# Attention's expert pieces: four raw buffers and loads two blocks ahead

## The reference, cut to what matters

```python
xn = _layernorm(x)
# spiking attention
Q, K, V = (spike(layer_norm(xn @ W.T + b, g, beta) - 1) for each of q, k, v)   # 16 heads of 16
attn = Dh - (q_sum + k_sum - 2 q k) + log_pe_bias(N, N)
out = spike(einsum(attn * scale, V) - 0.5)
attention = spike(layer_norm(out @ Wo.T + bo, go, betao) - 1)
# experts: 8, of which each token takes its best two
gate = renormalised top-2 of softmax(xn @ router_w.T)
experts = sum_e gate[e] * (silu(up_a) * up_b) @ down[e]
```

## Time and profile before

| | |
|---|---|
| three runs | 416.29 us median (415.83 to 416.88) |
| profiled execution | 416.35 us, of which 414.6 are the span from the first to the last instruction |
| TensorE busy | 364.6 us, 88% |
| TensorE weight loads | 298.1 us, 72% |
| VectorE busy | 271.8 us, 66% |
| GpSimd busy | 233.5 us, 56% |
| ScalarE busy | 225.4 us, 54% |
| granted clock of TensorE, mean | 0.957 (1.00 from 128 us to 400 us) |
| moved by the DMA engines | 51.72 MB, mean 125 GB/s |

### The profile page before, as it was taken

How to read it: one execution, slowest core, us unless ns; L and a number is a source line. 1 busy time by engine, 2 the same in 40 slices (tenths; PEclk the granted TensorE clock), 3 DMA queues, 4 the chain that set the end, 5 groups by cost and what they waited for, 6 DMA issues and landing times.

```text
span 414.6 us, 9181 instructions
## 1 busy us (share of the span) xinstructions
PE 364.6 (88%) x2421; PEld 298.1 (72%) x2430; DVE 271.8 (66%) x897; ACT 225.4 (54%) x716; POOL 233.5 (56%) x208
## 2 busy tenths in 40 slices
PE   5298976989999998988878999999999999999980
PEld 1233676988888856756667888888888888888860
DVE  4699799997776645856776555555555555555540
ACT  1456774777777654533444455555555555555540
POOL 4637423777777671644235657656555656565652
PEclk9589868999999999999999999999999999999996
DMA  7942012244534423466647566666666666665743
GB/s 264 323 155 77 25 51 53 104 156 130 176 136 162 159 104 102 146 197 212 174 142 227 81 113 102 102 102 103 102 102 101 103 100 104 99 105 93 112 52 38
DMA packets 43460, 51.72 MB, mean 125 GB/s; under 512 B 6342, under 2 KB 37064, under 8 KB 43432
## 3 DMA queue, kind: packets, MB, share of 16 engines
q0 software_dynamic: 13952, 19.30, 26.3%
q1 hardware_dynamic: 27488, 30.21, 24.5%
q10 hardware_dynamic: 1992, 1.89, 1.4%
HBM read 27.89 MB, written 23.48 MB: 124 GB/s over the span
## 4 chain that ended last, share of the span: by engine, by line
PE 54%; DVE 19%; issue 10%; POOL 6%; ACT 5%; DMA 4%; SPq 1%; POOLq 1%; DVEq 0%; ACTq 0%
PE bank L1137 15%; PE bank L1139 14%; PE bank L1138 14%; POOL rstd L704 4%; PE bank L1282 3%; PE bank L1264 3%; DMA xn<-x 3%; DVE qk_spk L1006 3%; DVE xn L808 2%; ACT junk L486 2%; DVE xst L786 2%; POOL slot_x L688 2%; PE bank L1203 1%; PE bank L1318 1%; DMA ex<-slot_x 1%
## 5 line engine op out<-in xcount | busy, mean ns | idle before, releaser
L737 POOL DMA_INDIRECT out<-ey,dest x71 | 110.0, 1549 | 72.4 <-ACT ey L547 25.5
L684 POOL DMA_INDIRECT slot_x<-xn,pos x64 | 62.8, 982 | 26.0 <-issue 20.2
L1037 DVE TENSOR_TENSOR hid<-gact,bank 128x256 f32<-128x256 f32 x71 | 29.9, 421 | 69.8 <-ACT gact L531 69.8
L1137 PE MATMUL bank<-ew,exT_h 128*128 x142 | 62.1, 438 | 2.7 <-DVE exT_l L975 2.6
L1137 PE MATMUL bank<-w_h,xT_h 128*128 128x256 f32 x192 | 59.5, 310 | 0.1
L1138 PE MATMUL bank<-w_l,xT_h 128*128 128x256 f32 x192 | 56.6, 295 | 0.0
L1139 PE MATMUL bank<-w_h,xT_l 128*128 128x256 f32 x192 | 56.4, 294 | 0.0
L1139 PE MATMUL bank<-ew,exT_l 128*128 x142 | 55.9, 393 | 0.0
L1138 PE MATMUL bank<-ew,exT_h 128*128 x142 | 55.8, 393 | 0.0
L531 ACT ACTIVATE gact<-bank 128x256 f32<-128x256 f32 x71 | 27.2, 384 | 51.3 <-PE bank L1139 51.3
L486 ACT ACTIVATE junk<-bank 128x256 bf16<-128x256 f32 x96 | 35.9, 380 | 28.9 <-PE bank L1139 28.9
(11 more groups left out here) (204 smaller groups left out, 891.1 us busy)
## 6 DMA issues: line engine op xcount, KB each, us to landing
ex<-slot_x SPq DMA_DIRECT2D x71, 130.0 KB, 2.5
ew_f<-experts SPq DMA_DIRECT2D x24, 256.0 KB, 3.1
xo<-x SPq DMA_DIRECT2D x16, 256.0 KB, 3.0
out<-xo SPq DMA_DIRECT2D x16, 256.0 KB, 3.4
xn<-x SPq DMA_DIRECT2D x6, 512.0 KB, 12.3
out<-ey,dest POOLq DMA_INDIRECT x71, 3.8
xn<-x SPq DMA_DIRECT2D x4, 256.0 KB, 3.7
w_f<-w_all ACTq DMA_DIRECT2D x1, 1024.0 KB, 7.9
```

Source lines behind the costliest of these rows:

```text
L684: pool.indirect_dma_start(slot_x, bass.IndirectOffsetOnAxis(ap=pos[:, k, t:t + 1], axis=0), xn[:, t, :], None).then_inc(s[done], 16)
L737: pool.indirect_dma_start(out, bass.IndirectOffsetOnAxis(ap=dest[:, j:j + 1], axis=0), ey[:, j % 4, :], None, compute_op=ALU.add).then_inc ...
L1037: v.tensor_tensor(hid[:, m % 2, :], gact[:, m % 2, :], h_ps[m % 2][:, F:2 * F], ALU.mult).then_inc(s["hid_done"], 1)
L1137: mm(dst, a_h, b_h, start=first, stop=False)
```

## The change

Attention's pieces get four raw places in place of two. The two new ones, `ew_more`, lie over the projections' weights; `ey` moves behind them, onto the old raw places. Pieces k 0, 1, 4, 5, 8 and 9 of attention use the old places, k 2, 3, 6 and 7 the new ones, each place with a semaphore of its own. SP issues k 0 in step 0 and k 1 in step 1 as before, k 2 and k 3 in step 2 after a wait for the last projection, k 4 and k 5 in step 3, and from step 4 on piece a+2 in step a; from k 4 on each waits until the piece four back is subtracted. All these issues stand in front of the step's wait for a store and its load of x, where `load_late` stood behind x.

```diff
+        ew_more = place_in(r_a)("ew_more", [P, 2, PW])
         ey = put("ey", [P, 4, D])
...
-        piece_in = [sem(f"piece_in{i}") for i in range(2)]
+        piece_in = [sem(f"piece_in{i}") for i in range(4)]
...
+        first_in_attention = POOL_PIECES + len(LATE_PIECES)
+
+        def raw_piece(n):
+
+            k = n - first_in_attention
+            if k >= 0 and k % 4 >= 2:
+                return ew_more[:, k % 2, :], piece_in[2 + k % 2], 16 * (k // 4 + 1)
+            earlier = n // 2 if k < 0 else first_in_attention // 2 + k // 4
+            return ew_f[:, n % 2, :], piece_in[n % 2], 16 * (earlier + 1)
...
+            def load_ahead(k):
+                n = ATTENTION_PIECES[k]
+                dst, done, _ = raw_piece(n)
+                if k < 2:
+                    sp.wait_ge(s["piece_l"], n - 1 - POOL_PIECES)
+                elif k >= 4:
+                    sp.wait_ge(s["piece_l"], n - 3 - POOL_PIECES)
+                sp.dma_start(dst, pieces[:, n]).then_inc(done, 16)
+
             sp.wait_ge(s["scattered_more"], 16 * TOPK * (FREED_MORE - FREED))
             for a in range(NB):
+                if a == 2:
+                    sp.wait_ge(s["proj_done"], G3 * NT)
+                for k in {0: [0], 1: [1], 2: [2, 3], 3: [4, 5]}.get(a, [a + 2]):
+                    if k in ATTENTION_PIECES:
+                        load_ahead(k)
                 if a >= 4:
                     sp.wait_ge(out_done[a % 4], 16 * (a // 4))
                 sp.dma_start(xo[:, a % 4, :, :], x_pairs[:, a, :, :]).then_inc(x_back[a % 4], 16)
-                if a in ATTENTION_PIECES:
-                    load_late(ATTENTION_PIECES[a])
                 if a >= 3:
                     store_block(a - 3)
...
             def piece_upper(n):
-                u = n % 2
+                raw, loaded, count = raw_piece(n)
...
-                act.wait_ge(piece_in[u], 16 * (n // 2 + 1))
-                nc.scalar.activation(piece(n, 0), ew_f[:, u, :], ACT.Copy).then_inc(s["piece_h"], 1)
+                act.wait_ge(loaded, count)
+                nc.scalar.activation(piece(n, 0), raw, ACT.Copy).then_inc(s["piece_h"], 1)
...
-                v.tensor_tensor(piece(n, 1), ew_f[:, m % 2, :], piece(n, 0).bitcast(F32), ALU.subtract).then_inc(s["piece_l"], 1)
+                v.tensor_tensor(piece(n, 1), raw_piece(n)[0], piece(n, 0).bitcast(F32), ALU.subtract).then_inc(s["piece_l"], 1)
```

## The result

Over seven runs of each, the changed kernel takes 410.99 us (median; 409.33 to 413.63) and the kernel before 415.83 (413.0 to 416.88). The ratio is 0.9891, with a 95% interval of 0.9855 to 0.9927: 4.5 us faster, between 3.0 and 6.0. The forecast was 411.5, range 410.6 to 413.2.

The account below looks back on a forecast made before the run. Late 256 KB piece loads, queued on SP behind a store's landing and x, were taken to hold ScalarE, VectorE and TensorE. Span 414.6 - 4.83 + 1.75 around it = 411.5 us; own range 410.6 to 412.4, given up to 413.2.

Parts of the forecast that it names:

- The four steps: Attention blocks 9 to 12: with no late piece, TensorE's steps shrink from 19.09 to 14.26 us, a gain of 4.83.
- The 0.85 at the end of attention: TensorE's idle time at 212.82, ascribed to the last blocks' own chain; none counted as gain, 0.85 possible at most.
- Two raw places over the weights, waits in front of x: SP queue: loads of k 2 and 3 wait for the last projection, x and stores behind moved waits; cost nothing.
- The landing of a store with a piece behind it: SP queue in attention: taken as 3.5 us, bounds 3.14 and 4.20; puts expert tile 4 at 212.1, cost 0 to 0.9.
- Ring order: Inside the DMA engines: by the skill's rule a piece behind a store would not hold it; landing 3.14, sum the same.
- L: The landing time of a store with a piece right behind it on the SP queue, taken as 3.5 us.
- The experts' stretch moves as a whole: Experts' 170 us, TensorE busy for 169.30: the stretch keeps its length and begins sooner.
- The rival in which SP's stores take the gain back: SP's out_done wait ahead of x becomes the bound, tile 4 turned 2.7 us later: 419.0 us, chance 0.05.

Follow-up runs that it names:

- the changed kernel's third profile: Changed kernel unchanged, run a second time in the experiments beside other kernels: 440.12 us against 446.14 for the kernel before, ratio 0.9855.
- the order alone: Kernel before with its two raw places; only the load of piece k moved in front of step k's store wait and load of x: ratio 0.9938.
- the lead alone: Changed kernel with four places and two blocks of lead, but piece loads behind x of their step: ratio 1.0012.
- The load behind the store: Kernel before, with the load of piece k behind the step's store instead of in front of it: ratio 0.9944.
- the end of attention tightened: VectorE's spike and tile parts reordered, tile 4 before the wait, zero rows earlier: on the changed kernel 0.9805; with two places and order alone 0.9804.
- VectorE's order at the end of attention: Changed kernel with block 15's spike before spike_out(12), and lower parts of expert tiles 0 and 1 before spike_out(13), on VectorE: ratio 0.9873.
- lead alone, tile 4 earlier: Four places and two-block lead with loads behind x, plus expert tile 4 issued in step 15 in front of the wait: ratio 0.9964.

## Why the prediction was right

- **The four steps.** Forecast 4.83 us from the earlier trace rows and 4.81 from the earlier trace rows; measured 4.84. All waits of L449 went, nothing took their place, VectorE and ScalarE had 2.9 and 2.0 us of work in steps of 3.6. The 0.85 at the end of attention stayed, 0.84 in the changed kernel, as forecast. It is less of a chain of its own than the prediction made it: the spike of block 15 stood on VectorE behind `spike_out` of block 12, which waits for the power, and with the spike in front the gap was gone.
- **Two raw places over the weights, waits in front of x.** Costed at nothing. Block 13 to the first expert matmul is 14.03 against 14.04 us; x of block 3 left at 162.19, in the time of the profile before 163.9, forecast near 164.
- **The landing of a store with a piece behind it.** Forecast 3.5 with 3.14 and 4.20 as ends; measured 2.87, 3.53 and 3.46. x of block 8 left at 183.57, which is 185.32 in the earlier profile's time, forecast 185.3. That it fits to the digit is luck: the three landings were 0.6 us shorter than forecast, the fourth, without a piece, 0.4 longer, and the times between an x and the next store 0.3 longer. From there to tile 4 were 27.5 us, not 26.8, since stores without a piece took up to 3.95 there; tile 4 left at 212.8 for the forecast 212.1. It landed in 3.7 us, as taken, and was turned at 215.33, which is 217.08 in the earlier time, forecast 217.1. So its wait stayed at nothing, but with half a microsecond to spare where the forecast had one; the changed kernel's third profile has 0.2 us of it.
- **Ring order.** The Trainium skill ("DMA: Bandwidth & Descriptors", section "Queues, rings and completion order") says that each DMA engine takes descriptors in ring order and that a completion count lands only after every earlier write of that engine. By that a piece behind a store does not hold it, and L would have been 3.14. Measured 2.87 to 3.53, a mean of 3.29, within the 2.75 to 3.95 of the stores with no piece about in the same kernel; the order alone had up to 3.91 with a piece behind. With a piece in front the lead alone had 3.72 to 5.15. The runs agree with it as far as these overlapping ranges can show.
- **The experts' stretch moves as a whole.** 198.3 to 199.4 us in the changed kernel against 198.8. Right.
- **The rival in which SP's stores take the gain back** is real, and its place, tile 4, was right. It did not decide the change, because the change also moved the piece behind the store; with the lead alone it decided, and gave back the whole 4.8 us. What its price left out is the clock: I counted the wait only, and behind the wait of 4.01 us the granted clock was 0.68 for 10 us.
- **The gain is the size forecast, the time is not evidence for the digits.** 4.5 us with 3.0 to 6.0 holds 4.83, and equally 3.5 or 5.5.
- **What I argued too simply**, without harm: that the late load was late by its place behind x alone. The load behind the store shows a second part, the pace of the queue, in which a piece in front of a store slowed the store that paced the next piece: with that gone 2.3 of the 4.8 us were back, though the load still stood behind x. The other 2.5 are its place behind the wait.
- **What the change did not need.** The prediction did not take the order apart from the two extra places and the second step of lead. The order alone gives the same four steps, and lead and places without the order give the same four steps and no time.

## What to carry to other kernels

In a queue of transfers, put what waits for nothing in front of what waits for a landing, and behind a store rather than ahead of it when the queue's next step waits for that store. A stall removed early is only kept if the next thing that this queue delivers also comes earlier: read off who is served last by it (here the fifth expert tile) before counting the gain. More buffers and more lead are worth trying only after the order; here two places gave the same four steps as four, and with the end of attention tightened the same time (0.9804 and 0.9805).

## What the runs showed of the hardware

- After TensorE stood 4.01 us for a load, it went on at the lower level of its clock, 1.2 GHz: the mean granted clock of the next 10 us was 0.68, and expert matmuls came 0.43 us apart instead of 0.23.
- The length of one idle time does not decide it. One of 2.00 us, with another of 0.90 behind it 5 us later (VectorE's order at the end of attention), left the clock at 1.00, and so did 1.62, 0.53, 0.92 and 1.10 us spread over four steps in the kernel before; 1.28, 1.06 and 0.71 us close together (lead alone, tile 4 earlier) were followed by matmuls 0.43 us apart, a mean of 0.83 over 10 us.
- The stores of blocks 1 to 3, 256 KB each, took 2.83 to 3.51 us with a piece issued behind them (changed kernel) and 3.73 to 5.15 us with a piece issued ahead of them (lead alone), on the same chip. The ranges of other blocks overlap: up to 3.91 with a piece behind (order alone), up to 3.95 with none about.
- The changed kernel took 411 us in its first runs and 440 to 441 us in the experiments, and the kernel before 416 and 446 to 448, with attention's steps equal to 0.01 us; the difference lay in the projections, where ScalarE stood still for over 5 us at a time. The cause is open, and whether it is the chip is not shown.
